# Maxima of the heads ahead of the rest of the q/k split on VectorE, in the units that hold both

## The reference: what is computed

```
h = modulate(norm(x));  q, k, v = split(h @ Wqkv + b)      # 16 heads of 9 dims
a = softmax(q k^T * 9**-0.5);  x = x + gate * ((a v) @ Wproj + b)
x = x + gate * mlp(modulate(norm(x)))
```

## Time and profile before

| | |
|---|---|
| median of 3 runs | 1541.4 us (1532.85 to 1543.26) |
| the profiled execution | 1537.86 us |
| its span | 1536.0 us |
| PE busy | 1409.2 us (92%) |
| PE weight loads busy | 1058.1 us (69%) |
| DVE busy | 1028.2 us (67%) |
| ACT busy | 781.9 us (51%) |
| POOL busy | 569.8 us (37%) |

### The profile page before, as it was taken

One profiled execution on the slowest core, in us unless ns is written; L12 is line 12 of the kernel. 1 busy time (PEld: TensorE's weight loads), 2 busy tenths in 40 slices (PEclk: granted clock), 3 DMA queues, 4 the chain that ended last, 5 costly groups with the idle time before them and its releaser, 6 DMA issues.

```text
span 1536.0 us, 41073 instructions
## 1 busy us (share of the span) xinstructions
PE 1409.2 (92%) x16016; PEld 1058.1 (69%) x16016; DVE 1028.2 (67%) x2537; ACT 781.9 (51%) x1290; POOL 569.8 (37%) x771
## 2 busy tenths in 40 slices
PE   5799988999999999999998867886999999999998
PEld 2377766777777776777777656665776677767776
DVE  4688876666776667888446668887546576666342
ACT  2377764333323336776555456665545366655543
POOL 3355542211131214554324345554324344333222
PEclk9799999999999999999999889999999899999999
DMA  4665631111022123554001234444115776774011
GB/s 129 156 155 145 166 93 53 51 44 44 36 68 73 25 82 98 142 144 115 18 32 39 71 107 112 103 108 119 29 41 72 130 108 114 143 128 94 28 51 47
DMA packets 209129, 134.94 MB, mean 88 GB/s; under 512 B 142461, under 2 KB 191320, under 8 KB 202730
## 3 DMA queue, kind: packets, MB, share of 16 engines
q1 hardware_dynamic: 188978, 129.74, 35.4%
q10 hardware_dynamic: 19960, 2.57, 1.2%
HBM read 98.24 MB, written 33.24 MB: 86 GB/s over the span
## 4 chain that ended last, share of the span: by engine, by line
PE 66%; DMA 11%; DVE 9%; issue 4%; SPq 4%; POOL 3%; ACT 2%; POOLq 0%; DVEq 0%; ACTq 0%
PE banks L979 9%; PE banks L962 8%; PE banks L999 7%; DMA qk<-qk_scr 7%; PE banks L950 6%; PE banks L685 5%; DVE negm L1569 4%; PE banks L651 4%; PE banks L669 3%; SPq L448 3%; PE banks L607 3%; PE banks L716 2%; PE banks L963 2%; PE banks L673 2%; PE banks L693 2%
## 5 line engine op out<-in xcount | busy, mean ns | idle before, releaser
L1569 DVE TENSOR_REDUCE negm<-banks 128x8 bf16<-128x1024 f32 x256 | 311.1, 1215 | 90.7 <-PE banks L651 88.7
L1262 ACT ACTIVATE prob<-banks 128x1024 f32<-128x1024 f32 x256 | 262.5, 1025 | 186.6 <-PE banks L673 183.7
L2026 POOL TENSOR_TENSOR X<-X,gx 128x288 f32<-128x288 f32 x128 | 104.3, 827 | 267.8 <-DVE gx L1599 266.1
L1393 ACT ACTIVATE hid<-banks 128x512 f32<-128x512 f32 x144 | 85.9, 597 | 219.5 <-PE banks L963 219.4
L979 PEld LDWEIGHTS banks<-wfc,hid 128*128 128x128 f32 x1152 | 156.7, 190 | 31.9 <-issue 20.1
L669 PE MATMUL banks<-qk 54*128 54x128 bf16 (+1 forms) x2048 | 169.5, 236 | 5.4 <-issue 3.3
L673 PE MATMUL banks<-mT,identb 64*128 64x128 bf16 x2048 | 166.2, 225 | 0.0
L979 PE MATMUL banks<-wfc,hid 128*128 128x144 f32 x1152 | 161.6, 286 | 1.7 <-DVE hid L1769 1.7
L651 PE MATMUL banks<-qk 54*128 54x128 bf16 (+1 forms) x2048 | 123.1, 242 | 38.0 <-DMA qk<-qk_scr 18.9
L962 PE MATMUL banks<-hT,wfc 128*128 128x512 f32 x288 | 148.6, 597 | 1.0 <-DVE hid L1481 0.5
L685 PE MATMUL banks<-prob,V 128*32 128x128 f32 x4096 | 145.8, 285 | 1.5 <-issue 1.5
(11 more groups left out here) (172 smaller groups left out, 2796.3 us busy)
## 6 DMA issues: line engine op xcount, KB each, us to landing
qk<-qk_scr SPq DMA_DIRECT2D x96, 216.0 KB
gbuf<-gate_scr SPq DMA_DIRECT2D x64, 288.0 KB, 4.6
qk_scr<-parts SPq DMA_DIRECT2D x48, 288.0 KB, 2.8
qk<-qk_scr SPq DMA_DIRECT2D x96, 144.0 KB
qk<-cw_scr SPq DMA_DIRECT2D x8, 1024.0 KB, 4.9
qk_scr<-parts SPq DMA_DIRECT2D x48, 144.0 KB, 2.4
qk<-qk_scr SPq DMA_DIRECT2D x96, 72.0 KB
qk<-tok_scr SPq DMA_DIRECT2D x32, 216.0 KB
```

The source lines that it names most:

```text
L1262: act.activation(prob[:, 2 * (U % 3):2 * (U % 3) + 2, :], pairs[1][:], ACT.Exp, scale=scale).then_inc(a_exp, 1)
L1569: dve.tensor_reduce(negm[:, u // 2, :, 4 * (u % 2):4 * (u % 2) + 4], pairs[0][:].rearrange("q s (h k) -> q s h k", k=T), AX.X, ALU.max, ne ...
L2026: pool.tensor_tensor(x, x, gx[:, q, :, :], ALU.add).then_inc(g_x, 1)
```

## The change

In DVE's stream the two lines that take the maxima are moved ahead of the two that take the rest. It touches units in which both stand: three units (1 to 3, in layer 2 3 to 5) of steps 0 to 5 in each of four layers, so 72 of the 256 units. No instruction, wait or semaphore is added or removed on any engine; no other stream changes.

```diff
@@ -1657,10 +1657,10 @@
                         U = UNITS * n + u
                         if u % 2 == 1 and U + 3 < last:
                             max_out((U + 3) // 2)
+                        if U + AHEAD < last:
+                            head_max(l, U + AHEAD)
                         if q0 < u <= q0 + 3 and g < 6:
                             rest1(n + 2, u - q0 - 1, 6)
-                        if U + AHEAD < last:
-                            head_max(l, U + AHEAD)
                         if u % 2 == 0 and (g or u):
                             normed(U // 2 - 1)
```

## The result

The changed kernel takes 1558.35 us, the median of 4 runs (1552.28 to 1561.92); the kernel before, now with 4 runs, 1537.83 us. By the bound of 1% it is a slowdown, which had a chance of 0.38; the interval's lower end, 0.9%, lies just inside the bound, and "within 1%" had 0.57. The +18 us stand on the border between the forecast (+9 to +18) and the rival that loses clock (+18 to +28). The profiled execution took 1557.19 us, its span 1555.3, against 1537.86 and 1536.0. PE's mean granted clock is 0.970, before 0.969.

The account below looks back on a forecast made before the run. PE's chain through DVE and POOL was taken to bound layers 0 and 1, a rest-to-arrival transfer loop layer 2, SP's queue and read layer 3. Terms 4.3 + 3.9 + 4.5 + 0.3 = 13.0 us gave 1553 us, range 1542 to 1566.

Parts of the forecast that it names:

- the forecast (+9 to +18): Whole kernel: the moved rest delays PE and layer 2's arrivals, 13.0 us in sum; chance 0.56.
- the rival that loses clock: Layer 2: longer waits make two or three more starts at 1.2 GHz, 2.6 us each; +18 to +28, chance 0.18.
- 8.2 forecast: Layers 0 and 1: PE's later blocks and layer 0's later transfers, 3.9 us in layer 0 and 4.3 in layer 1.
- the 0.37 us of unit 2: Layers 0 and 1, unit 2: block 2 starts 0.67 us later, `turn_max` absorbs 0.30, 0.37 goes on.
- 0.1, which I count at nothing: Layer 1, step 2, unit 1: block 1 can start at 630.62 against 630.51, taken as no delay.
- the 2 x 1.6 for layer 0's transfers: Layer 0: two just-in-time transfers come as late as block 2's rest, so two step pairs lose 1.6 us each.
- over a microsecond ahead of need in layer 1: Layer 1: the read arrives early enough that the rest moved 1.6 us later in unit 3 costs nothing.
- 4.5 forecast: Layer 2: the last rest, in unit 5, makes six arrivals 0.9 us later each, 5.4, partly absorbed to 4.5 us.
- 0.3 forecast: Layer 3: SP's issues, not the rest, set the read; 0.05 us a step, 0.3 us in all.
- maxima would start near 1284.55: Layer 3: the rest then starts at 1285.76 and block 2 at 1286.50 against 1286.48, hardly later.
- Covered: Rival, whole kernel: the rest's spare time hides the shift, only part of layer 2 remains; -3 to +8 us, chance 0.21.
- Faster: Rival, whole kernel: earlier maxima fill DVE's idle time before the 72 rests; 16 to 24 us gained, chance 0.05.

Follow-up runs that it names:

- The first swap: Kernel before with the two instructions exchanged only in the first of the three units (unit 1, in layer 2 unit 3): 1.0037 [1.0021, 1.0052], +5.7 us.
- the third swap alone: Kernel before with the exchange only in the third unit (unit 3, in layer 2 unit 5): 1.0069 [1.0043, 1.0094], +10.6 us.
- the early rest: Kernel before with layer 2's last rest moved from unit 5 to the end of unit 4, ahead of the statistics: 0.9970 [0.9947, 0.9992].
- the wait on POOL: Changed kernel, POOL's two parts of block 0 held until `hr` is written, except in layer 2: 1.0078 and, again, 1.0106 to the kernel before.
- the second swap alone: Kernel before with the exchange only in the second unit (unit 2, in layer 2 unit 4): 1.0018 [1.0001, 1.0036], +2.8 us.

## Why the prediction came out as it did

The time fell in the range and 5 us above the forecast, and the forecast causes, PE's wait for the moved rest and layer 2's later arrivals, are there. But by swaps the sum is off in each: 2.1, 4.0 and 6.9 us forecast, 5.7, 2.8 and 10.6 measured. That the total is near is in part luck. By its steps:

*Layers 0 and 1, 8.2 forecast, 9.4 [6.5, 12.3] measured, the composition wrong.* The mechanism holds: PE waits for the moved rest ahead of blocks 1 and 2 (layer 0: 8 waits, 7.2 us; layer 1: 10 waits, 5.7 us), `turn_max` behind block 2 no longer, and the 0.37 us of unit 2 are met to 0.01 wherever `hr` keeps its length. Block 2 waits in all twelve steps, 0.42 to 1.55 us (forecast 0.6 to 1.1), and block 1 in four of layer 1, as counted, and in two of layer 0. Two terms were off, one too low and one too high, so that their sum fits by luck. "0.1, which I count at nothing" for unit 1 looked at PE's block 1 alone. The same rest also releases POOL, whose line 1999 then ran beside `hr`; five of the twelve waits of block 2 are the 1.12 us of the step shown above, and the 1.55 of layer 0's first step has a stretched `hr` too. The first swap costs 5.7 us over all layers, for which I had 2.1; how much of that is the overlap stays open, between nothing and 6 us. And the 2 x 1.6 for layer 0's transfers has no counterpart: with the third swap alone, layer 0's stretch was 158.7 us. The read "over a microsecond ahead of need in layer 1" was not: with that swap alone PE waits 0.7, 0.2 and 0.7 us for arrivals there, though that layer's stretch is no longer either (156.6).

*Layer 2, 4.5 forecast; 4.6 by difference.* The form of the loop is shown from both sides: the third swap alone makes its step starts 1.1 us further apart, the early rest brings them 0.95 nearer (5.7 over six) and gains 4.6 us. In the whole change the same six steps take 178.5 and 176.9 us in its two profiles, and 177.3 and 182.0 with the wait on POOL, which is not in layer 2; in the four profiles in which layer 2 is as before they take 176.1 to 176.9. That is 0.3 more for each step in the mean, not 0.9; and PE's waits for arrivals in layer 2 went from 14.5 to 16.5, not 18. The first two swaps seem to give something back here: with the first or the second alone layer 2's stretch is 205.9 and 205.2 us, under the 207.1 to 209.2 of the four profiles in which nothing is changed there, with the third alone 214.2. These are single profiles, and the four of the changed layer 2 lie from 207.1 to 214.3 themselves, so the size of this term is only the difference of medians, 4.6 with some 5 either way; that it meets 4.5 says little.

*Layer 3, 0.3 forecast, 3.7 [0.5, 6.9] measured: the mis-sized term.* The step that failed is "maxima would start near 1284.55, [...] block 2 at 1286.50 against 1286.48". Three things are missing in it. It takes the scores to be ready 0.44 us after their first matmul, which is a row of layer 2; in layer 3 the eight matmuls have 62 rows and last 0.64 us, and DVE starts 0.67 us after them (1295.50 - 1294.83). It sets a start in the timeline beside one in the chain: in the timeline of the kernel before, block 2 starts at 1286.32, so that 1286.50 meant 0.18, not 0.02. Together the two give 0.41 us; with the second swap alone `turn_max` comes 0.43 later. And `hr` at 1.48 us beside POOL adds 0.31. Since block 2 is here followed by work that waits for nothing, the whole 0.74 goes on. That SP's issues set the read is true and did not protect PE's block. The line of PE's timeline of the kernel before:

```profile
1286.32 1.02 PE L607 MATMUL banks<-hT,wqkv 128*96 128x512 f32 x2
```

*The rivals.* Covered: fallen, 24 waits of 16.4 us stand at line 607. Faster: fallen, the waits for maxima sank by 0.6 us. More clock lost: fallen as a sum (0.970 against 0.969), though single starts changed places, as they do between two profiles of the kernel before. The time of that rival, 1557 to 1561, was met by another cause.

## What to carry over

An instruction moved back on an in-order engine must be followed to each of its readers, not only to the one on the busiest engine: here the swap whose wait on the busiest engine looked like nothing cost 5.7 us, and the helper engine that it releases was pushed onto an unrelated instruction and stretched it. Read how long an operand takes to be ready from rows of the same stage and shape. If the trace shows a loop that is closed through one instruction and a transfer, try that instruction earlier before anything else: no other edit here gained.

## What the runs showed of the hardware

DVE's `hr` has two inputs in SBUF. Beside a POOL operation that also reads SBUF, one of the two waits for the other, as these traces show. `hr`, 64x512 f32, takes 0.74 us alone, up to 1.71 beside line 1999, up to 1.11 beside line 1997 and 1.36 to 1.86 beside POOL's scaling (line 2013); it is 0.73 to 0.74 again when POOL is made to wait. In all 16 overlaps of the kernel before and in 23 of the 24 of the changed one, `hr` ends 0.54 to 0.55 us after the POOL operation beside which it started, whenever it started; the one left began 0.15 us before POOL's end and took its 0.74. The other way round POOL pays. From the changed kernel, layer 0, step 1:

```profile
96.30 0.61 POOL L1997 CAST parts<-res 96x512 bf16<-96x512 f32 x1 [2.81 <-DVE res L1530]
96.57 0.88 DVE L1523 SCALAR_TENSOR_TENSOR hr<-hhi,masks,hmod 64x512 fp32r<-64x512 f32 x1 [0.41 <-ACT hhi L1213]
97.00 1.48 POOL L1999 TENSOR_TENSOR parts<-res,parts 96x512 bf16<-96x512 f32 x1
```

`hr` waits for line 1997 and is under way when line 1999 starts, which then takes 1.48 us instead of 1.16; beside `hr` this occurs five times (1.47 to 1.49). The Trainium skill ("GPSIMD Engine Reference", "Key points") says that GpSimd shares its SBUF interfaces with VectorE and that they contend when VectorE's instruction has two SBUF inputs; the trace agrees. The rest (line 1530), with one input in PSUM, kept 0.65 to 0.69 us, beside POOL's operations (18 of 96) as well as alone.
